# Pairing half of the third window's h before the other half is copied, in an octonion feed-forward kernel

## The chip, the cores and the metric

The kernel runs on one core of a Trainium2 chip. The metric is the device time of one execution in microseconds (us). The engines are TensorE (PE, matmuls), VectorE (DVE), ScalarE (ACT), GpSimd (POOL), and SyncE (SP), which here only issues DMAs. Each engine works through its own instructions in order; between engines there are semaphores.

## The reference

The input x has 32 sequences of 64 rows with 1024 features. Each sequence picks one of 16 matrices of 64x64, which mixes its 64 rows. The result y goes through a feed-forward layer with weights that are quantised to -1, 0 and 1 times a scale and that act as octonion products (8 parts of 128 features; the hidden width is 2728, 8 parts of 341), and x is added at the end:

```python
def oct_ternary_linear(xp, W):
    Wq = ternary_dequant(W)
    M = jnp.einsum('jik,jod->koid', S_OCT, Wq)
    return jnp.einsum('...id,koid->...ko', xp, M)
...
y = einsum('bct,bcd->bdt', x, weights[condition])
gate = oct_ternary_linear(y, w_gate); up = oct_ternary_linear(y, w_up)
h = jax.nn.silu(gate) * up
x = x + oct_ternary_linear(h, w_down)
```

## The kernel before, in words

The 2048 rows are worked through in 8 tiles T of 256 rows. The 341 hidden rows of a part are cut into three windows w of 128, 128 and 85. A tile has 12 chunks c (4 per window); a chunk makes the h of two of the eight octonion parts (v = 0 and v = 1) for one window. Chunks 8 to 11 are the third window. Every operand of the big matmuls is split into two fp16 values, a high part (ACT) and a low part (DVE).

**Gate and up.** For each chunk PE multiplies y with the gate and up tables (L1240, in the third window L1248), DVE adds the shared parts, ACT applies the silu, DVE makes h (L1083, L1047). In the third window the product comes out with rows and columns exchanged, so PE turns h (turn, L1304) two chunks later. ACT then copies h twice (split_h): the high part into h_op (L762), and the fp32 value into h_f (L767), which counts the semaphore h_copied up by one per chunk. DVE makes the low part of h (h_lo, L988).

**Rounds of z.** The down product needs, beside h itself, sums of h, called z. There are six rounds k per tile: k = 2w + v takes the four chunks of window w, half v. pair_up (L469) forms four pairings of 256 columns, of chunks 0 and 1 of the window (a = 0) and of chunks 2 and 3 (a = 1), each as a sum and a difference (r0 = 0, 1); two of them go out as one instruction of 512 columns where the signs agree, which they do for v = 1 and not for v = 0 (of the first window and the third, among others). Then two instructions of 512 columns form the sum and the difference of the pairings (L684, L685). All these are tensor_tensor instructions that a helper records at L617 on POOL and at L895 on DVE. POOL does rounds 0 to 4 of each tile (round_of_z, L672). It waits for the copy of all four chunks of the window (h_copied, L674), for the end of its last round (z_ready, L676), then pairs; it waits for the pairings (L678) and for z's buffer z_f to be free (z_lo_ready, L680), then makes z. Round 5 is done by DVE (last_round_of_z, L997), with the buffers pu_sb and z_dve. ACT makes z's high part (z_hi, L782), DVE its low part (z_lo, L995). In tiles 0 to 6 both take round 4 first and round 5 then; in the last tile round 5 first (last_rounds, L461).

**Order at the end of a tile.** ACT: the copies of chunks 10 and 11, the high part of the next tile's y (y_hi, L746), z_hi of the last two rounds, then a copy out of the down product's banks (L832). DVE: z_lo of round 3, h_lo of chunks 10 and 11, round 5, z_lo of rounds 4 and 5, the low part of the next y (y_lo, L979), the scaled addition of the down product to the residual (add_down, L1093, counts c_added), then mix_down (L1108, counts wd_ready). PE (down, L1440): for both halves s of the rows the products of windows 0 and 1 with h (down_c) and z (down_u), then those of the third window, z's last, all recorded at L1401. Then comes the next tile's first chunk (own, L1329), which writes the banks that add_down reads and so waits for c_added (L1333). In the last tile (last_down, L1414) PE does z's part of the third window and then, for the second half, all products with h. POOL ends a tile with back (L528), which adds the mixed parts to the output in SBUF; SP stores it and loads the next residual. In tile 0 POOL also mixes weights and sums y ahead of round 4 (L698 to L701).

The wait for z at the third window's product is L1465 (L1432 in the last tile); for rounds 0 to 3, z_lo_ready is awaited at L1456 (L1424).

Of the kernel before, what the change touches and what calls it, by code (L numbers as in the profile page):

```python
# [75 lines left out]
def parity(n):  # L76

    return -1 if bin(n).count("1") % 2 else 1
# [81 lines left out]
def build(nc, x, cond, cond_w, w_gate, w_up, w_down, out, count):  # L160
# [7 lines left out]
    NC = len(CHUNKS)  # L168
    NU = NC // 2
    NR = 2 * NQ  # L170
# [56 lines left out]
    with ExitStack() as ctx:  # L227
        def sb(name, shape, dt):
            return ctx.enter_context(nc.sbuf_tensor(name, shape, dt))

        def sem(name):
            return ctx.enter_context(nc.semaphore(name))
# [11 lines left out]
        h_pairs = sb("h_pairs", [P, 2, 2, TOK], F32)  # L244
# [193 lines left out]
        h_copied = sem("h_copied")  # L438
        h_lo_ready = sem("h_lo_ready")
        pairs_ready = sem("pairs_ready")  # L440
        z_ready = sem("z_ready")
# [24 lines left out]
        def z_of(k):  # L466
            return (z_dve if k == NR - 1 else z_f)[0:ROWS[k // 2]]

        def pair_up(add, k, pairs):  # L469
            w, v = divmod(k, 2)  # L470
            n_rows = ROWS[w]
            for r0 in range(2):
                signs = [KAPPA[2 * a + 1 + 4 * v] * parity(r0) for a in range(2)]
                a_runs = [(slice(0, 2), signs[0])] if signs[0] == signs[1] else [
                    (slice(a, a + 1), signs[a]) for a in range(2)]
                for a, sign in a_runs:
                    c = 4 * w + 2 * a.start
                    n = a.stop - a.start
                    op = add(pairs[0:n_rows, a, r0, :], h_f[0:n_rows, c:c + 2 * n - 1:2, v, :],
                             h_f[0:n_rows, c + 1:c + 2 * n:2, v, :], sign)  # L480
            return op
# [122 lines left out]
        def _(pool):  # L604
# [11 lines left out]
            def signed_add(dst, a, b, sign):  # L616
                return pool.tensor_tensor(dst, a, b, ALU.add if sign > 0 else ALU.subtract)  # L617
# [53 lines left out]

            def round_of_z(T, k):  # L672
                n = (NR - 1) * T + k
                pool.wait_ge(h_copied, NC * T + 4 * (k // 2) + 4)  # L674
                if n > 0:
                    pool.wait_ge(z_ready, n)  # L676
                pair_up(signed_add, k, h_pairs).then_inc(pairs_ready, 1)
                pool.wait_ge(pairs_ready, n + 1)  # L678
                if k > 0:
                    pool.wait_ge(z_lo_ready, NR * T + k)  # L680
                elif T > 0:
                    pool.wait_ge(z_lo_ready, NR * T)
                z, pairs = z_of(k), h_pairs[0:ROWS[k // 2]]
                signed_add(z[:, 0:2], pairs[:, 0], pairs[:, 1], 1)  # L684
                signed_add(z[:, 2:4], pairs[:, 0], pairs[:, 1], -1).then_inc(z_ready, 1)  # L685
# [4 lines left out]
            for T in range(NT):  # L690
                if T > 0:
                    for s in range(SUB):
                        back(pool, T - 1, s)
                if T == 0:
                    mix_down_weights(0)
                    mix_down_weights(1)
                    pool.wait_ge(slots_built[1], NQ * NBUILD)
                    for k in range(4):  # L698
                        round_of_z(T, k)
                    sum_y(1)  # L700
                    round_of_z(T, 4)  # L701
                    continue
                if T + 1 < NT:
                    sum_squares(T + 1)
                round_of_z(T, 0)
                round_of_z(T, 1)
                if T + 1 < NT:
                    sum_y(T + 1)
                for k in range(2, NR - 1):
                    round_of_z(T, k)  # L710
# [182 lines left out]
        def _(dve):  # L893
# [103 lines left out]
            def last_round_of_z(T):  # L997
                dve.wait_ge(h_copied, NC * (T + 1))
                dve.wait_ge(h_ready, NC * (T + 1))
                pair_up(signed_add, NR - 1, pu_sb).then_inc(pairs_ready_dve, 1)  # L1000
                dve.wait_ge(pairs_ready_dve, T + 1)
                z, pairs = z_of(NR - 1), pu_sb[0:LAST]
                signed_add(z[:, 0:2], pairs[:, 0], pairs[:, 1], 1)
                signed_add(z[:, 2:4], pairs[:, 0], pairs[:, 1], -1).then_inc(z_ready_dve, 1)
# [525 lines left out]
```

## Time and profile before

| what | us |
|---|---|
| median of 3 runs | 682.19 |
| lowest and highest run | 680.11, 682.54 |
| the profiled execution | 679.68 |
| its span, first to last instruction | 677.9 |
| PE busy | 639.2 (94%) |
| DVE busy | 513.9 (76%) |
| POOL busy | 386.0 (57%) |
| ACT busy | 323.6 (48%) |
| mean granted clock of PE | 0.993 |

A busy time is the time in which the engine has an instruction under way. Matmuls overlap, so a busy PE is one with no gap that shows. A row of a timeline has the start, the time taken, the engine, the line, the operation, what it writes and reads, how often, and in brackets the idle time before it and what ended that.

### The profile page before, as it was taken

How to read it: one execution, taken by the hardware profiler on the slowest of the kernel's cores; microseconds unless marked ns; L12 is line 12 of the kernel's file. 1: busy time of each engine (PE TensorE's matmuls, PEld its weight loads, DVE VectorE, ACT ScalarE, POOL GpSimd, SP SyncE). 2: the span in 40 equal slices, each digit the busy share in tenths (PEclk: the TensorE clock that was granted, in tenths of full speed). 3: DMA queues.
4: the chain of work that ended last, by engine and by line, in shares of the span. 5: the costliest groups of instructions: out<-in, count | busy, mean ns of one | idle time of the engine just before them, and what ended most of it. 6: DMA issues, size and time to landing. Idle time of an engine off the chain costs nothing. (4 is left out here: it accounts for less than half of the span.)

```text
span 677.9 us, 17119 instructions
## 1 busy us (share of the span) xinstructions
PE 639.2 (94%) x7010; PEld 592.4 (87%) x7010; DVE 513.9 (76%) x873; ACT 323.6 (48%) x542; POOL 386.0 (57%) x453
## 2 busy tenths in 40 slices
PE   3599988899999999999999999999999999999995
PEld 3378888799999999998998999999999989988995
DVE  1899975868877687767878687767878688787786
ACT  4847545255544546254553455355452544535441
POOL 1256397547647576358656476375863486464563
PEclk9799999999999999999999999999999999999999
DMA  8200030040002200032001300032000300011001
GB/s 344 67 2 1 1 131 1 33 159 3 2 1 95 99 2 1 2 125 67 2 2 42 150 2 2 1 105 88 1 2 3 125 1 2 2 62 64 2 1 63
DMA packets 10576, 31.50 MB, mean 46 GB/s; under 512 B 3330, under 2 KB 3330, under 8 KB 10370
## 3 DMA queue, kind: packets, MB, share of 16 engines
q1 hardware_dynamic: 9906, 28.81, 12.1%
q10 hardware_dynamic: 592, 1.61, 0.7%
q8 instruction: 55, 0.90, 0.5%
q14 instruction: 23, 0.19, 0.1%
HBM read 22.02 MB, written 8.39 MB: 45 GB/s over the span
## 5 line engine op out<-in xcount | busy, mean ns | idle before, releaser
L1240 PE MATMUL ps<-y_op,gate_table 128*128 128x256 f16 x1408 | 181.5, 274 | 10.7 <-DVE y_op L979 4.2
L1240 PE MATMUL ps<-y_op,up_table 128*128 128x256 f16 x1408 | 179.8, 273 | 0.3 <-ACT up_table L724 0.3
L1240 PEld LDWEIGHTS ps<-y_op,gate_table 128*128 128x128 f16 x1408 | 137.6, 98 | 29.6 <-issue 6.1
L617 POOL TENSOR_TENSOR h_pairs<-h_f 128x256 f32<-128x256 f32 (+2 forms) x128 | 119.8, 965 | 67.5 <-ACT h_f L767 54.6
L1240 PEld LDWEIGHTS ps<-y_op,up_table 128*128 128x128 f16 x1408 | 137.7, 98 | 16.6 <-DVE up_table L895 0.7
L524 POOL TENSOR_TENSOR o_sb<-o_sb,wd_sb 128x256 f32<-128x256 f32 (+1 forms) x150 | 87.5, 619 | 89.7 <-DVE wd_sb L1108 88.6
L617 POOL TENSOR_TENSOR z_f<-h_pairs 128x512 f32<-128x512 f32 (+1 forms) x80 | 102.2, 1298 | 36.5 <-DVE z_op L995 34.5
L1248 PE MATMUL ps<-third_table,y_op 128*128 128x170 f16 x1408 | 108.2, 237 | 0.5 <-ACT third_table L724 0.5
L1248 PEld LDWEIGHTS ps<-third_table,y_op 128*128 128x128 f16 x1408 | 105.1, 97 | 1.0 <-issue 0.7
L822 ACT ACTIVATE ps<-ps,small 128x512 f32<-128x512 f32 x64 | 42.4, 662 | 107.6 <-DVE ps L1009 81.6
L1401 PE MATMUL ps<-down_u,z_op 128*128 128x256 f16 (+1 forms) x768 | 90.1, 273 | 3.3 <-DVE z_op L995 3.3
L1401 PE MATMUL ps<-down_c,h_op 128*128 128x128 f16 (+1 forms) x1536 | 92.1, 219 | 1.1 <-DVE pu_sb L1047 1.1
L1401 PEld LDWEIGHTS ps<-down_c,h_op 128*128 128x128 f16 (+1 forms) x1536 | 88.8, 98 | 1.9 <-issue 1.3
L895 DVE TENSOR_TENSOR pu_sb<-ps,q_sb 128x170 f32<-128x170 f32 (+1 forms) x128 | 64.8, 506 | 33.5 <-PE ps L1240 14.2
L1401 PEld LDWEIGHTS ps<-down_u,z_op 128*128 128x128 f16 (+1 forms) x768 | 73.8, 98 | 11.7 <-DVE z_op L995 3.8
L988 DVE TENSOR_TENSOR h_op<-ps,h_op 128x512 f16<-128x512 f32 (+1 forms) x96 | 65.7, 685 | 21.8 <-ACT h_f L767 21.7
L995 DVE TENSOR_TENSOR z_op<-z_f,z_op 128x1024 f16<-128x1024 f32 (+1 forms) x40 | 49.6, 1240 | 38.9 <-ACT z_op L782 38.8
L762 ACT ACTIVATE h_op<-ps 128x512 f16<-128x512 f32 (+1 forms) x96 | 57.3, 597 | 31.1 <-DVE ps L1083 30.6
L782 ACT ACTIVATE z_op<-z_f 128x1024 f16<-128x1024 f32 (+1 forms) x40 | 42.1, 1054 | 36.4 <-POOL z_f L617 36.4
L767 ACT ACTIVATE h_f<-ps 128x512 f32<-128x512 f32 (+1 forms) x96 | 57.6, 600 | 0.0
L1083 DVE SCALAR_TENSOR_TENSOR ps<-pu_sb,small,ps 128x512 f32<-128x512 f32 x64 | 48.3, 755 | 8.1 <-ACT ps L822 2.0
L1009 DVE TENSOR_TENSOR pu_sb<-ps,pu_sb 128x512 f32<-128x512 f32 x48 | 32.9, 685 | 19.5 <-PE ps L1240 19.4
(98 smaller groups left out, 640.6 us busy)
## 6 DMA issues: line engine op xcount, KB each, us to landing
x_in<-in_x_dram SPq DMA_DIRECT2D x8, 1024.0 KB, 5.2
o_sb<-in_x_dram SPq DMA_DIRECT2D x16, 512.0 KB, 3.6
out_dram<-o_sb SPq DMA_DIRECT2D x15, 512.0 KB, 2.7
h_op<-in_L_ffn_w_gate_dram ACTq DMA_DIRECT2D x3, 512.0 KB, 6.6
h_op<-in_L_ffn_w_up_dram SPq DMA_DIRECT2D x3, 512.0 KB, 7.3
z_op<-in_L_ffn_w_down_dram SPq DMA_DIRECT2D x1, 1536.0 KB, 11.3
out_dram<-o_sb SPq DMA_DIRECT2D x2, 256.0 KB, 3.1
cond_bd<-in_L_cond_weights_dram SPq DMA_DIRECT2D x30, 16.0 KB, 2.9
```

The source lines that it names most:

```text
L524: last = eng.tensor_tensor(dst, dst, wd_sb[:, s, k1, r0, h, :], ALU.add if sign > 0 else ALU.subtract)
L617: return pool.tensor_tensor(dst, a, b, ALU.add if sign > 0 else ALU.subtract)
L762: act.activation(h_op[rows, c, :, 0, :], h_bank(c), ACT.Copy).then_inc(h_hi_ready, 1)
L767: act.activation(h_f[rows, c], h_bank(c), ACT.Copy).then_inc(h_copied, 1)
L822: act.activation(bank_r(s, 0), bank_r(s, 0), ACT.Silu, scale=gate_scale(T)).then_inc(silu_ready, 1)
L895: return dve.tensor_tensor(dst, a, b, ALU.add if sign > 0 else ALU.subtract)
L988: dve.tensor_tensor(h_op[rows, c, :, 1, :], h_bank(c), h_op[rows, c, :, 0, :], ALU.subtract).then_inc(h_lo_ready, 1)
L995: dve.tensor_tensor(z_op[rows, k, 1], z_of(k), z_op[rows, k, 0], ALU.subtract).then_inc(z_lo_ready, 1)
L1083: dve.scalar_tensor_tensor(out=bank_r(s, 0), in0=u_sb[:], scalar=up_scale(T), in1=bank_r(s, 0), op0=ALU.mult, op1=ALU.mult).then_inc(h_rea ...
L1240: mm = pe.matmul(dst, table[m][:, slot, q, :], y_op[:, op, e, :], start=(i == 0 and e == 0), stop=(i == len(terms) - 1 and e == 1))
L1248: mm = pe.matmul(dst, y_op[:, op, e, P * s:P * s + P], third_table[:, slot].rearrange("p m r -> p (m r)"), start=(i == 0 and e == 0), stop ...
L1401: mm = pe.matmul(banks[bank][:, place], operand[:, P * s:P * s + P], weights, start=(bank not in begun), stop=(last and i == ends[bank]), ...
```

## The change

In round k = NR - 2 = 4 (the third window, v = 0) POOL waits for the copy of the first two of the window's four chunks and for its last round's end, pairs those two chunks (a = 0, two instructions), then waits for the last two chunks and pairs them (a = 1, two instructions). pair_up takes the parts to do as an argument. All other rounds stay, and so does DVE's round 5.

```diff
-        def pair_up(add, k, pairs):
+        def pair_up(add, k, pairs, parts=(0, 1)):
             w, v = divmod(k, 2)
             n_rows = ROWS[w]
             for r0 in range(2):
                 signs = [KAPPA[2 * a + 1 + 4 * v] * parity(r0) for a in range(2)]
-                a_runs = [(slice(0, 2), signs[0])] if signs[0] == signs[1] else [
-                    (slice(a, a + 1), signs[a]) for a in range(2)]
+                a_runs = [(slice(0, 2), signs[0])] if signs[0] == signs[1] and len(parts) == 2 else [
+                    (slice(a, a + 1), signs[a]) for a in parts]
...
             def round_of_z(T, k):
                 n = (NR - 1) * T + k
-                pool.wait_ge(h_copied, NC * T + 4 * (k // 2) + 4)
-                if n > 0:
+                if k == NR - 2:
+
+                    pool.wait_ge(h_copied, NC * T + NC - 2)
                     pool.wait_ge(z_ready, n)
-                pair_up(signed_add, k, h_pairs).then_inc(pairs_ready, 1)
+                    pair_up(signed_add, k, h_pairs, (0,))
+                    pool.wait_ge(h_copied, NC * T + NC)
+                    pair_up(signed_add, k, h_pairs, (1,)).then_inc(pairs_ready, 1)
+                else:
+                    pool.wait_ge(h_copied, NC * T + 4 * (k // 2) + 4)
+                    if n > 0:
+                        pool.wait_ge(z_ready, n)
+                    pair_up(signed_add, k, h_pairs).then_inc(pairs_ready, 1)
                 pool.wait_ge(pairs_ready, n + 1)
```

## Rows read from the trace of the kernel before

**Rows 1.** The page, its first part: busy us (share of the span) and instructions.
```profile
PE 639.2 (94%) x7010; PEld 592.4 (87%) x7010; DVE 513.9 (76%) x873; ACT 323.6 (48%) x542; POOL 386.0 (57%) x453
```

**Rows 2.** Waits of PE, from 150 to 643 us, then from 643: total, times, longest.
```profile
PE ps L1240 <- issue: 1.2, 6, 0.2
...
PE ps L1401 <- DVE z_op L995: 2.0, 1, 2.0
```

**Rows 3.** Timeline of PE at the end of tile 6: start, us, engine, line, operation.
```profile
579.22 1.91 PE L1401 MATMUL ps<-down_u,z_op 128*128 128x256 f16 x16
...
591.61 3.66 PE L1401 MATMUL ps<-down_u,z_op 85*128 85x256 f16 x32
595.47 1.91 PE L1240 MATMUL ps<-y_op,gate_table 128*128 128x256 f16 x16 [0.20 <-issue]
```

**Rows 4.** Timeline of DVE at the end of tile 6.
```profile
587.57 1.22 DVE L995 TENSOR_TENSOR z_op<-z_f,z_op 85x1024 f16<-85x1024 f32 x1 [3.47 <-ACT z_op L782]
...
593.97 1.40 DVE L1093 SCALAR_TENSOR_TENSOR o_sb<-ps,small,o_sb 128x512 f32<-128x512 f32 x2
```

**Rows 5.** Timeline of ACT in tile 6: the copy of chunk 9, z_hi of round 4.
```profile
572.23 0.58 ACT L767 ACTIVATE h_f<-ps 85x512 f32<-85x512 f32 x1
...
586.48 1.06 ACT L782 ACTIVATE z_op<-z_f 85x1024 f16<-85x1024 f32 x1 [3.64 <-POOL z_f L617]
```

**Rows 6.** Timeline of POOL in tile 6, z of round 3, then round 4.
```profile
573.78 2.50 POOL L617 TENSOR_TENSOR z_f<-h_pairs 128x512 f32<-128x512 f32 x2 [3.07 <-DVE z_op L995]
...
579.38 0.72 POOL L617 TENSOR_TENSOR h_pairs<-h_f 85x256 f32<-85x256 f32 x1 [3.10 <-ACT h_f L767]
...
580.07 1.22 POOL L617 TENSOR_TENSOR h_pairs<-h_f 85x256 f32<-85x256 f32 x1
...
582.38 1.17 POOL L617 TENSOR_TENSOR h_pairs<-h_f 85x256 f32<-85x256 f32 x1
...
583.63 1.60 POOL L617 TENSOR_TENSOR z_f<-h_pairs 85x512 f32<-85x512 f32 x1
...
585.19 1.26 POOL L617 TENSOR_TENSOR z_f<-h_pairs 85x512 f32<-85x512 f32 x1
```

**Rows 7.** Timeline of DVE in tile 6, from z_lo of round 3 to round 5.
```profile
577.40 1.23 DVE L995 TENSOR_TENSOR z_op<-z_f,z_op 128x1024 f16<-128x1024 f32 x1 [0.87 <-ACT z_op L782]
...
579.40 0.69 DVE L988 TENSOR_TENSOR h_op<-ps,h_op 85x512 f16<-85x512 f32 x1 [0.18 <-ACT h_f L767]
580.01 0.68 DVE L895 TENSOR_TENSOR pu_sb<-h_f 85x512 f32<-85x512 f32 x1
...
580.61 1.22 DVE L895 TENSOR_TENSOR pu_sb<-h_f 85x512 f32<-85x512 f32 x1
...
582.89 1.21 DVE L895 TENSOR_TENSOR h_f<-pu_sb 85x512 f32<-85x512 f32 x1
```

**Rows 8.** Timelines at the end of tile 0: ACT's last copy, POOL's round 4, PE.
```profile
105.40 0.60 ACT L767 ACTIVATE h_f<-ps 85x512 f32<-85x512 f32 x1
...
108.45 4.13 POOL L617 TENSOR_TENSOR h_pairs<-h_f 85x256 f32<-85x256 f32 x4
...
124.16 1.91 PE L1240 MATMUL ps<-y_op,gate_table 128*128 128x256 f16 x16 [1.82 <-issue]
```

**Rows 9.** The last tile: chain of waits (first row, start, us, what), then timelines.
```profile
653.61 0.02 POOLq L680
...
657.88 2.84 POOL L617 TENSOR_TENSOR z_f<-h_pairs 85x512 f32<-85x512 f32 x2
...
658.39 1.06 ACT L782 ACTIVATE z_op<-h_f 85x1024 f16<-85x1024 f32 x1 [4.82 <-DVE h_f L895]
...
659.48 2.32 DVE L995 TENSOR_TENSOR z_op<-h_f,z_op 85x1024 f16<-85x1024 f32 x1 [1.12 <-ACT z_op L782]
661.84 1.22 DVE L995 TENSOR_TENSOR z_op<-z_f,z_op 85x1024 f16<-85x1024 f32 x1
...
663.12 3.67 PE L1401 MATMUL ps<-down_u,z_op 85*128 85x256 f16 x32 [1.95 <-DVE z_op L995]
```

## The prediction

> **What bounds the kernel now.** I read the page first: TensorE (PE) is busy for 639.2 us, 94% of a span of 677.9 us [rows 1]. So only time in which PE stands still can be saved. The view of waits, for PE alone and by stretch, says where that is behind the first tile: between 150 and 643 us it idles six times by 0.2 us, at the first matmul of a tile (L1240), and in the last stretch once by 2.0 us, for VectorE's (DVE's) z_op, the low part of z (L995) [rows 2]. The first tile has its own gaps, among them 1.82 us before tile 1. The six short gaps are one pattern, once per tile; I follow the one ahead of the last tile.
>
> The gap of 0.20 us counts from the modelled end of the last matmul. Sixteen such matmuls of 0.273 us take 1.91 us, so one follows another by (1.91 - 0.27) / 15 = 0.109 us; the 32 from 591.61 would make room for the next at 595.10, and it starts at 595.47 [rows 3]. **Each gap is really worth 0.37 us**, and the wait of 1.95 us in the last tile 1.95 + 0.27 - 0.11 = 2.11 us.
>
> What ends the short gap the trace calls "issue". I read it from DVE's timeline: the low parts of z from 587.57, behind them y's low parts, and behind those, up against them, the residual's first addition, at 593.97 + 1.40 = 595.37, 0.10 us before PE goes on [rows 4]. In the code L1333 has PE wait for just this (c_added), since the addition reads the banks that the next tile's first chunk writes. DVE had come late because it stood idle up to 587.57 for ScalarE's (ACT's) copy at 586.48, and ACT had waited 3.64 us for POOL's z [rows 4, 5]. So POOL's round 4 sets the tile's border.
>
> **What the change moves.** Round 4 has four pairings of 85x256 and two z instructions of 85x512, before and after; the two signs differ for v = 0, so no run is split by the new parts. Only their order changes, and one wait more stands between the second and third pairing. Chunk 9 is copied at 572.23 + 0.58 = 572.81 [rows 5]. POOL's z of round 3 ends at 573.78 + 2.50 = 576.28, then it idles until the copy of chunk 11 releases it at 579.38 [rows 6]. Two pairings fit into that hole: from 576.36, 0.72 us for one, they end at about 577.8.
>
> They do not simply come off the path, because **POOL and DVE take turns** in instructions that read two operands from SBUF. Look at 580 us: DVE's pairing runs 580.01 to 580.69, POOL's, started at 580.07, ends at 581.29, that is 0.60 us after DVE's; DVE's next, started at 580.61, ends at 581.83, 0.54 us after POOL's. POOL's pairing to 583.55, DVE's to 584.10, POOL's z to 585.23 [rows 6, 7]: each time the later one ends its own working time (POOL 0.59 for a pairing, 1.13 for a z; DVE 0.55) after the other has finished. In the last tile DVE's z_lo, 1.22 us when alone, takes 2.32, and ends 1.08 us after POOL's z does at 660.72 [rows 9].
>
> With these turns I lay out a middle tile:
> - POOL: pairings 1 and 2 in the hole; 3 from 579.38 to 580.10, 4 to 581.29 as the second one now; then z at once, from 581.37, held to 581.83, done 582.96; second z, held by DVE to 583.51, done **584.64 instead of 586.45**: 1.8 us earlier, where two pairings as they stand are 1.17 each, 2.3 us.
> - DVE's own last round (k = 5): its third and fourth instruction are now held by z instructions of 1.13 instead of pairings of 0.59. They end at 583.51 and **585.19 instead of 584.10**: 1.1 us later. ACT's copy of round 4 (from 584.68) hides that: round 5's comes about 1 us after it.
> - DVE then starts z_lo of round 4 at 585.8 instead of 587.57, and the addition ends at 593.6, well before PE's 595.10. The gap closes; the cap is PE itself, so of 1.8 us only 0.37 counts. Six borders: **-2.2 us** (0.20 x 6 = 1.2 is the least, if my reading of the modelled ends is off).
> - Cost on the way: z_lo of round 3 (577.40) is held to 577.8 and ends at 578.85 instead of 578.63. PE needs it at 579.22 [rows 3, 7]: a margin of 0.37 us covers it, 0 us. If the cover goes, each later tenth costs a tenth in each of six tiles. The low part of h behind it reads PSUM; the one at 579.40 was not held by the pairing at 579.38 [rows 6, 7].
> - The added wait costs POOL an instruction of its own at most, and the chain of waits has one at 0.02 us [rows 9]. Queued behind it are POOL's last two pairings and z, with ACT and DVE behind those, which needed chunk 11 before too. 0 us, at most 0.1 on the last tile's path. No DMA is issued or passed by POOL; the stores on SP's queue come 1 to 2 us earlier and nobody waits for them.
> - The first tile: chunk 11 is copied by 106.0, and POOL, late with other sums, begins round 4 at 108.45. Both waits are passed there, only the order changes; the 1.82 us before tile 1 stays [rows 8]. 0 us, within 0.1 either way for one more wait.
>
> **The last tile** is where the chain of waits runs through POOL, and where one expects the most. But there DVE finishes round 5 first (last_rounds is reversed). The same turns, 74.25 us later (from 583.63 to 657.88, where POOL's z starts): DVE's round ends at 659.44 instead of 658.35, ACT's copy of it 660.55 instead of 659.45 [rows 6, 9]. POOL is done by 658.9, so DVE's z_lo at 660.58 is no longer held: 1.22 us instead of 2.32, it ends at 661.80, exactly as before. Round 4's copy by ACT is over by 661.6; its z_lo can start right behind, at 661.72 instead of 661.84. Gain: **-0.1 us** of the 2.11. The bounds are +1.1 (the round lost, nothing given back) and -2.11 (the wait gone).
>
> The Trainium skill has a rule that speaks against a gain here: "SBUF — State Buffer", section "Who interferes with whom", has the pair of ports that VectorE and GpSimd share as an exclusive lock for a whole instruction, taken by whoever issues first, when VectorE has two SBUF inputs. By that rule the last tile gives nothing, as the durations in this trace do; were it a split of bandwidth it would give 1.2 us.
>
> **Sum.** -2.2 - 0.1 = -2.3 us. The profiled execution took 679.68 us (span 677.9), so 677.4 by it. That execution lay 2.5 us below the median of the three runs, 682.19 (they reach from 680.11); the same difference from the median gives **679.9 us**. About 0.5%, 3.4 us, is what a measurement of this kernel can tell from no change: the forecast is within it.
>
> **Rivals.**
> 1. *The last tile gains too.* DVE gets its turns sooner than I have it, its round ends at 658.4 and its z_lo at 660.7, then 661.9: 1.2 us off, up to 2.1. For it: the chain that ended last goes through all four pairings and both z. Against: strict turns in every pair of rows. Sum -3.4 to -4.3: 678.8 to 677.9 us. Chance 0.16.
> 2. *Nothing moves.* The trace names no releaser of the six gaps; were it PE's own start of the new tile, DVE's 1.8 us would be hidden. Against: the end of the addition leads PE by 0.10 us, and the code has the wait. Or the early pairings never start early, since z_ready comes with the end of round 3: only if that wait lasts to 579. 682.1 us. Chance 0.14.
> 3. *Slower: DVE loses its turn and POOL wins nothing.* If POOL's z still ends near 660 in the last tile (because of the added wait, or of its pairings being held by z_lo of round 3), DVE's round 5 ends 1.1 us later, its z_lo is still held, and PE waits 1.1 us longer, while the borders stay open: 683.3 us. It decides from the point where POOL's last z ends later than 660.6, when z_lo starts. Against: the hole is 3.1 us for 1.4 us of work. Chance 0.08. Slower by over 0.5% needs, on top of it, z_lo of round 3 past its margin of 0.37 us in all tiles.
>
> My forecast keeps 0.62. Faster by over 0.5%: most of rival 1 and a little scatter, 0.20; slower by over 0.5%: 0.04; within: 0.76. Range: from 677.6 (rival 1, and a little scatter) to 682.6 (rival 2 and half of rival 3's loss).
>
> **What would show it.** Right: POOL's pairings in two groups of two, the first from about 576.4 in the tile that I followed; z done 1.8 us earlier; PE's six idle times of 0.2 us gone from its waits, and each tile from the second on 0.37 us shorter; DVE's round 5 ending 1.1 us later; and in the last tile PE still idle for about 1.9 us ahead of the down product of z. Wrong: the last idle time down to 1 us or less (rival 1), the six gaps in place (rival 2), a new wait of PE for DVE's z_lo in the second window's product (the margin was not enough).

## The result and the profile after

The changed kernel takes 679.7 us (median of 22 runs, 676.87 to 680.7), the kernel before, run beside it, 681.11 (22 runs). The ratio is 0.9976 with a 95% interval of 0.9968 to 0.9984: 1.6 us faster, between 1.1 and 2.2, and within the 0.5% that the prediction called no change. The forecast was 679.9 us, 2.3 us off a median of 682.19.

A run's mean granted clock of PE is the clock that the chip granted it, as a share of the full 2.4 GHz, averaged over the run. It is on record for 64 runs of the kernel before (those beside the experiments below, and its repetition) and for the 22 of the changed kernel, and the runs fall into groups by it. The groups are a better ruler than the medians (one slow run of the kernel before, 690.48 us at a clock of 0.941, is left out):

| mean granted clock | before: runs, us | median | changed: runs, us | median |
|---|---|---|---|---|
| 0.981 to 0.982 | 19, 681.6 to 682.9 | 682.0 | 11, 679.3 to 680.7 | 680.1 |
| 0.985 to 0.987 | 9, 681.2 to 683.4 | 681.7 | 3, 679.5 to 679.8 | 679.8 |
| 0.988 to 0.991 | 28, 679.6 to 680.9 | 680.4 | 8, 676.9 to 678.5 | 678.2 |
| 0.993 | 8, 679.4 to 679.8 | 679.6 | none | |

Within a group the change is worth about 1.9 to 2.2 us, though the clocks of the two kernels in a group are close and mostly not the same. What a kernel's median is depends also on how its runs spread over the groups.

**The borders between the tiles.** In the view of waits of PE, from 150 to 643 us, the changed kernel has no row at all: the six idle times of 0.2 us [rows 2] are gone. Its timelines at the end of tile 6 (start, us, engine, line, operation; lines from L682 on are 8 higher than before), POOL first:

```profile
573.68 2.50 POOL L617 TENSOR_TENSOR z_f<-h_pairs 128x512 f32<-128x512 f32 x2 [3.07 <-DVE z_op L1003]
576.33 1.41 POOL L617 TENSOR_TENSOR h_pairs<-h_f 85x256 f32<-85x256 f32 x2
579.28 1.92 POOL L617 TENSOR_TENSOR h_pairs<-h_f 85x256 f32<-85x256 f32 x2 [1.54 <-ACT h_f L775]
581.28 3.28 POOL L617 TENSOR_TENSOR z_f<-h_pairs 85x512 f32<-85x512 f32 x2
...
577.30 1.52 DVE L1003 TENSOR_TENSOR z_op<-z_f,z_op 128x1024 f16<-128x1024 f32 x1 [0.88 <-ACT z_op L790]
...
581.79 3.33 DVE L903 TENSOR_TENSOR h_f<-pu_sb 85x512 f32<-85x512 f32 x2
585.69 1.22 DVE L1003 TENSOR_TENSOR z_op<-z_f,z_op 85x1024 f16<-85x1024 f32 x1 [0.58 <-ACT z_op L790]
...
592.09 1.40 DVE L1101 SCALAR_TENSOR_TENSOR o_sb<-ps,small,o_sb 128x512 f32<-128x512 f32 x2
...
591.51 3.66 PE L1409 MATMUL ps<-down_u,z_op 85*128 85x256 f16 x32
595.00 1.91 PE L1248 MATMUL ps<-y_op,gate_table 128*128 128x256 f16 x16
```

This execution is 0.10 us ahead of the one before here (PE's z product at 591.51 for 591.61, [rows 3]). POOL's pairings stand in two groups, with the hole between them. z is done at 581.28 + 3.28 = 584.56 for 586.45, DVE's round 5 at 585.12 for 584.10, and the addition, up to 595.37 before [rows 4], ends at 593.49. PE goes on at 595.00, 3.49 us after 591.51: 32 times 0.109, no gap.

What the six gaps gave can be read from the two traces directly. From the second group of products of tile 1, where both are at full clock, to the first of tile 7 the kernel before takes 595.47 - 125.91 = 469.56 us, with this row as its start, and the changed one 595.00 - 127.61 = 467.39: 2.17 us less, six times 0.36.

```profile
125.91 1.91 PE L1240 MATMUL ps<-y_op,up_table 128*128 128x256 f16 x16
```

**The last tile.** The same views:

```profile
653.18 1.91 POOL L617 TENSOR_TENSOR h_pairs<-h_f 85x256 f32<-85x256 f32 x2 [1.55 <-ACT h_f L775]
655.17 3.27 POOL L617 TENSOR_TENSOR z_f<-h_pairs 85x512 f32<-85x512 f32 x2
...
655.68 3.31 DVE L903 TENSOR_TENSOR h_f<-pu_sb 85x512 f32<-85x512 f32 x2
660.11 1.22 DVE L1003 TENSOR_TENSOR z_op<-h_f,z_op 85x1024 f16<-85x1024 f32 x1 [1.12 <-ACT z_op L790]
661.25 1.21 DVE L1003 TENSOR_TENSOR z_op<-z_f,z_op 85x1024 f16<-85x1024 f32 x1
...
658.75 1.95 PE L1409 MATMUL ps<-down_c,h_op 85*128 85x128 f16 x32
662.53 6.16 PE L1409 MATMUL ps<-down_u,z_op 85*128 85x256 f16 x32 [1.82 <-DVE z_op L1003]
668.48 6.39 PE L1409 MATMUL ps<-down_c,h_op 128*128 128x128 f16 x96
```

z_lo of round 5 runs in 1.22 us instead of 2.32 [rows 9], but DVE's z of round 5 takes 3.31 instead of 2.2, and PE still idles for 1.82 us, where it idled for 1.95. POOL's z is done at 655.17 + 3.27 = 658.44, where it was 660.72; this execution is 0.46 us ahead at the copy of chunk 11 (POOL starts at 653.18, before at 653.64), so 1.8 us of that are the change's. The last tile hardly gains by it.

The last two rows hold what the prediction did not have: PE's 32 products take 6.16 us, before 3.67 [rows 9]. The view by stretches, from 662 to 670 us, gives the granted clock (the 0.59; busy times of PE, PEld, DVE, ACT, POOL before it), between the full 2.4 GHz and 1.2; before it was 1.00 there:

```profile
662.00:670.00 8.00, 7.47 (x47) 5.92 (x48) 3.70 (x6) 1.37 (x2) 2.36 (x4) 0.59 0.01 2
```

The clock was low at the start of tile 1 as well (0.76 in the stretch from 123 to 130 us, before 1.00). There the first 16 products take 3.50 us:

```profile
124.28 3.50 PE L1248 MATMUL ps<-y_op,gate_table 128*128 128x256 f16 x16 [1.82 <-issue]
127.61 1.91 PE L1248 MATMUL ps<-y_op,up_table 128*128 128x256 f16 x16
```

Both have a price. The first is 3.33 us from 124.28 to 127.61 for the 1.75 that such a group takes at full clock (595.00 to 596.75), 1.6 us. The second shows from the start of z's product to the end of the span: 678.3 - 662.53 = 15.8 us, before 677.9 - 663.12 = 14.8, so 1.0 us. The profiled execution took 680.12 us; less 2.6 that is 677.5, where the prediction had 677.4. A third low stretch, 0.83 from 100 to 110 us (before 1.00), costs little: tile 1 starts at 124.28 for 124.16.

### The profile page after: what moved, and what is told of

Read it like the earlier page. It is cut to its first block and busy times, and to the rows that moved or that the text cites. A ratio compares the mean times of both kernels' runs of the same rounds, so it can differ in the third digit from the quotient of the medians.

```text
span 678.3 us, 17119 instructions
## 1 busy us (share of the span) xinstructions
PE 644.8 (95%) x7010; PEld 596.8 (88%) x7010; DVE 522.1 (77%) x873; ACT 323.3 (48%) x542; POOL 383.2 (56%) x453
## 5 line engine op out<-in xcount | busy, mean ns | idle before, releaser
L617 POOL TENSOR_TENSOR h_pairs<-h_f 128x256 f32<-128x256 f32 (+2 forms) x128 | 113.9, 916 | 59.0 <-ACT h_f L775 45.1
L617 POOL TENSOR_TENSOR z_f<-h_pairs 128x512 f32<-128x512 f32 (+1 forms) x80 | 105.3, 1336 | 36.6 <-DVE z_op L1003 34.7
L1409 PE MATMUL ps<-down_u,z_op 128*128 128x256 f16 (+1 forms) x768 | 93.3, 278 | 1.8 <-DVE z_op L1003 1.8
L1409 PE MATMUL ps<-down_c,h_op 128*128 128x128 f16 (+1 forms) x1536 | 94.0, 221 | 1.1 <-DVE pu_sb L1055 1.1
L1409 PEld LDWEIGHTS ps<-down_c,h_op 128*128 128x128 f16 (+1 forms) x1536 | 90.6, 99 | 2.0 <-issue 1.3
L1409 PEld LDWEIGHTS ps<-down_u,z_op 128*128 128x128 f16 (+1 forms) x768 | 75.3, 100 | 11.5 <-DVE z_op L1003 2.0
L1003 DVE TENSOR_TENSOR z_op<-z_f,z_op 128x1024 f16<-128x1024 f32 (+1 forms) x40 | 51.7, 1291 | 21.4 <-ACT z_op L790 21.4
```

The lines of the kernel that those rows point to most:

```text
L1003: dve.tensor_tensor(z_op[rows, k, 1], z_of(k), z_op[rows, k, 0], ALU.subtract).then_inc(z_lo_ready, 1)
L1409: mm = pe.matmul(banks[bank][:, place], operand[:, P * s:P * s + P], weights, start=(bank not in begun), stop=(last and i == ends[bank]), ...
```

## The experiments

My theory A: six borders give 0.37 us each, because DVE's addition comes earlier; the last tile gives nothing, because POOL and DVE take turns. The rivals: B, the last tile gives the time; C, the low clock belongs to the new order; D, PE waits at the border for something else, or the change has a gain beside the gaps; E, POOL is slow in the last tile for itself; F, against C, the clock falls now and then in either kernel. Ratios are to the kernel before, run beside them.

**Where the gain is: the change cut in two.**

```diff
-                if k == NR - 2:
+                if k == NR - 2 and T == NT - 1:
```

> The changed kernel with the new order of round 4 in the last tile alone. Theory A (the gain is at the six tile borders, the last tile gives nothing because POOL and DVE take turns): ratio 0.9995 to 1.000, 0 to 0.1 us; PE's six idle times of 0.20 us stay; in the last tile POOL's pairings stand in two groups, DVE's round 5 ends about 1.1 us later, PE still idles 1.8 to 2.0 us before z's last product. Theory B (the last tile gives what the change saves, 1.2 to 2.1 us): ratio 0.997 to 0.998, PE's idle time there under 1 us.

Measured: 679.96 us, 0.9984 (0.9973 to 0.9996). The waits of PE between 150 and 640 us keep the gaps, and the last tile looks as in the changed kernel.

```profile
PE ps L1248 <- issue: 1.2, 6, 0.2
```

The timelines of its last tile:

```profile
652.99 1.91 POOL L617 TENSOR_TENSOR h_pairs<-h_f 85x256 f32<-85x256 f32 x2 [1.55 <-ACT h_f L775]
...
655.49 3.31 DVE L903 TENSOR_TENSOR h_f<-pu_sb 85x512 f32<-85x512 f32 x2
...
662.34 5.50 PE L1409 MATMUL ps<-down_u,z_op 85*128 85x256 f16 x32 [1.82 <-DVE z_op L1003]
```

Theory A's trace, and 0.13 us of idle time gained. The ratio is lower than expected, and its interval reaches B's 0.997 to 0.998: none of its 12 runs had a clock of 0.982, and 9 of the 21 of the kernel before had. Runs of 0.990 are 679.95 to 680.27 against 680.12 to 680.52, and the medians at 0.986, 0.990 and 0.993 lie about 0.3 us apart. B is out by the trace, which has 1.82 us of idle time where B had under 1, and by these runs.

```diff
-                if k == NR - 2:
+                if k == NR - 2 and T < NT - 1:
```

> The changed kernel with the new order of round 4 in every tile but the last. Theory A: all of the gain, 2.2 us, ratio 0.9968; the six idle times of PE at the start of a tile are gone, the last tile is as before (POOL's four pairings in one group, PE idle for 1.95 us). Theory B: less than 1 us, ratio over 0.9985. Theory C (a lower granted clock at the end or after tile 0 comes with the new order and eats part of the gain): if it hangs on the last tile's new order, the clock near the end is full again here.

Measured: 679.75 us, 0.9974 (0.9963 to 0.9985), the whole of the change's gain; a little less than the 2.2 us that I expected, within the interval. No idle row between 150 and 640 us. In the last tile POOL works as before and the clock falls all the same:

```profile
652.48 4.16 POOL L617 TENSOR_TENSOR h_pairs<-h_f 85x256 f32<-85x256 f32 x4 [3.10 <-ACT h_f L775]
...
661.94 6.43 PE L1409 MATMUL ps<-down_u,z_op 85*128 85x256 f16 x32 [1.94 <-DVE z_op L1003]
```

So the fall does not hang on the last tile's new order.

```diff
-                if k == NR - 2:
+                if k == NR - 2 and T > 0:
```

> The changed kernel with the new order of round 4 in tiles 1 to 7, tile 0 as before. Theory A (tile 0 gets nothing from the change, since chunk 11 is copied long before POOL comes to round 4): the same as the changed kernel, ratio 0.9966 to 0.9976. Theory C (the falls of PE's granted clock at about 103 and 124 us in the changed kernel's trace come from tile 0's new order): they are gone here, and the ratio is 0.2% lower.

Measured: 678.54 us, 0.9967 (0.995 to 0.9983); the changed kernel's interval overlaps it. In this execution the clock was full from 100 to 110 us and at the start of tile 1, and low at the end (0.50 from 662 to 670). But among its 11 runs are three with a clock of 0.981 or 0.982, at 679.46 to 680.49, like the changed kernel's. One full stretch in one execution doesn't decide on C, and the times don't tell it apart; the next run says more.

**Does the low clock belong to the change?** The kernel before, once more:

> The kernel before once more, for a second trace and for the scatter. Theory F (the granted clock falls at the same few places in any of these kernels, now and then): ratio 1.000 within 0.001; the six idle times of 0.20 us are there again; and if this execution is one with a lower mean clock than 0.993, the falls stand near 103 to 127 us and after 660 us, as in the changed kernel. Theory C (those falls belong to the change): none there.

Measured: 680.86 us, 1.0001 (0.9986 to 1.0016). Its profiled execution took 681.71 us, at a mean clock of 0.982. The view of waits from 150 to 640:

```profile
PE ps L1240 <- issue: 1.1, 6, 0.2
```

PE's timeline in the last tile, and after it the view of the stretch from 662 to 670:

```profile
662.54 7.01 PE L1401 MATMUL ps<-down_u,z_op 85*128 85x256 f16 x32 [1.95 <-DVE z_op L995]
```

```profile
662.00:670.00 8.00, 7.46 (x39) 5.50 (x40) 3.21 (x5) 1.10 (x2) 1.49 (x3) 0.53 0.01 2
```

The same code, after the same wait of 1.95 us, ran these products in 3.67 us the first time and in 7.01 now. The view of 100 to 110 us has 0.83, as the changed kernel's has. So the low clock at these two places is met in either kernel, and C is out for them; what decides between low and full is open. At the start of tile 1 this execution had the full clock. Of the traces in which PE idles for 1.82 us there, three of the five with the new order in tile 0 have the low clock behind it, and none of the four without. Of the changed kernel's 22 runs 11 are in the slowest group of the table and none in the fastest, of the kernel before 19 and 8 of 64. Both point to falls that come more often with the change; neither settles it.

**Is it the addition that PE waits for at a border?** DVE's addition moved ahead, POOL untouched (in the kernel before):

```diff
-                    y_lo(T + 1)
-                if T + 1 < NT:
-                    for s in range(SUB):
-                        add_down(T, s)
+                    y_lo(T + 1, range(2))
+                    add_down(T, 0)
+                    y_lo(T + 1, range(2, NY))
+                    add_down(T, 1)
```

> The kernel before, with DVE's first addition of the down product moved ahead of the last third of y's low part; POOL as before. Theory A (PE's idle time at a tile border waits for that addition, 0.37 us at six borders, and at the border after tile 0 most of 1.98 us): the addition ends 1.8 us earlier, all seven gaps close, 2.2 + 1.7 = 3.9 us, ratio 0.9943. Theory D (PE waits there for y or for something of its own): the gaps stay, ratio 1.000.

Measured: 676.51 us, 0.9926 (0.9912 to 0.994). In the waits from 100 us on, all seven gaps at L1241 are missing; the second fence has the timelines of DVE and PE at the first border:

```profile
PE ps L1305 <- DVE odd_h_sb L1047: 2.1, 1, 2.1
PE ps L1402 <- DVE z_op L995: 1.9, 1, 1.9
```

```profile
121.22 1.40 DVE L1093 SCALAR_TENSOR_TENSOR o_sb<-ps,small,o_sb 128x512 f32<-128x512 f32 x2
122.53 1.80 DVE L979 SCALAR_TENSOR_TENSOR y_op<-y_f,small,y_op 128x1536 f16<-128x1536 f32 x1
...
122.72 1.91 PE L1241 MATMUL ps<-y_op,gate_table 128*128 128x256 f16 x16
```

PE starts tile 1 at 122.72, 0.10 us after the addition's end, where it did at 124.16 [rows 8]. It isn't y that it waited for: y's last third (DVE's row from 122.53) is under way when PE starts, up to 124.33. D's first half is out: PE waits for this addition. Two runs at a clock of 0.993 took 675.55 and 675.63 us, 4.0 less than the kernel before at that clock, for the 3.9 expected. The ratio itself says 5.0 us, more than the 0.9943 expected: at the lower clocks the difference is larger, 676.06 us against 680.12 to 680.52 at 0.990, and 676.96 to 677.16 at 0.984 against 681.63 to 682.38 at 0.982.

The same edit in the changed kernel:

> The changed kernel with DVE's first addition moved ahead of the last third of y's low part. Theory A (both edits close the same six gaps, which can be closed but once): against the kernel with that addition moved alone (ratio 0.9926) only the last tile's 0.1 us are added, ratio 0.992 to 0.993. Theory D (the change has a gain of its own beside the gaps): another 1.5 to 2 us, ratio 0.990.

Measured: 676.2 us, 0.9946 (0.9925 to 0.9966), five runs spread over four clocks; the 0.992 to 0.993 that I expected is at the interval's edge. At 0.993 it took 675.31, 0.2 to 0.3 us less than the same edit without the change, and at 0.990 676.2 for 676.06. The gaps can be closed only once: beside the moved addition the change is worth next to nothing, and D's second half, another 1.5 to 2 us, is out.

**Are the turns real?** DVE's round 5 taken out of the last tile (z of round 5 isn't computed there; one instruction of one column stands for it):

```diff
+                if T == NT - 1:
+                    dve.tensor_scalar(warm_dve, scale[0], 1.0, None, ALU.mult).then_inc(z_ready_dve, 1)
+                    return
                 pair_up(signed_add, NR - 1, pu_sb).then_inc(pairs_ready_dve, 1)
```

> The changed kernel without DVE's round 5 in the last tile (four instructions left out, one of one column in their place; z of round 5 there is not computed). Theory A (turns between POOL and DVE): POOL's last pairing takes 0.72 us instead of 1.2, its two z instructions 2.5 us together instead of 3.27, so z of round 4 is done 1.2 us earlier after chunk 11's copy (4.0 us instead of 5.3), and z_lo runs in 1.22 us. PE's idle time before z's last product falls from 1.8 to under 0.2 us. Theory E (POOL is slow there for itself, by its own waits): POOL's times stay at 1.2 and 3.27.

Measured: 677.2 us in a single run. The timelines:

```profile
653.28 1.41 POOL L618 TENSOR_TENSOR h_pairs<-h_f 85x256 f32<-85x256 f32 x2 [1.54 <-ACT h_f L776]
654.77 3.47 POOL L618 TENSOR_TENSOR z_f<-h_pairs 85x512 f32<-85x512 f32 x2
...
655.21 1.91 DVE L1004 TENSOR_TENSOR z_op<-h_f,z_op 85x1024 f16<-85x1024 f32 x1 [1.12 <-ACT z_op L791]
...
658.85 1.95 PE L1413 MATMUL ps<-down_c,h_op 85*128 85x128 f16 x32
660.64 3.67 PE L1413 MATMUL ps<-down_u,z_op 85*128 85x256 f16 x32
```

The pairings take 1.41 us instead of 1.91: alone, they are 0.7 each. POOL's z did not fall to 2.5 us as I had written: with round 5 gone, z_lo of round 5 came forward, to 655.21, took its turn between the two z instructions, and was itself held, 1.91 us instead of 1.22. A miss of my expectation (POOL's z is done 5.0 us after chunk 11's copy, not 4.0), and one more instance of turns: here z_lo holds POOL's z as round 5 did. POOL slow for itself (E) is out, by the pairings. PE's wait before z is gone.

**The last tile's order.** Round 4 first there too:

```diff
-            return ks if T + 1 < NT else ks[::-1]
+            return ks
```

> The changed kernel, with ACT and DVE taking round 4 ahead of round 5 in the last tile too. Theory A, by the turns laid out from the trace: ACT copies round 4's z about 0.5 us before DVE's round 5 ends, DVE's two low parts end about 0.5 us earlier, PE idles about 1.3 us instead of 1.8 there: 0.5 us better than the changed kernel, ratio to the kernel before 0.9960 at equal clock. Theory B (DVE's round 5 is what PE waits for, whatever the order): no difference from the changed kernel, idle 1.8 us.

Measured: 677.51 us, 0.996 (0.9945 to 0.9976). The timelines of the last tile:

```profile
653.54 3.31 DVE L903 TENSOR_TENSOR h_f<-pu_sb 85x512 f32<-85x512 f32 x2
657.42 1.22 DVE L1003 TENSOR_TENSOR z_op<-z_f,z_op 85x1024 f16<-85x1024 f32 x1 [0.57 <-ACT z_op L790]
...
659.83 3.67 PE L1409 MATMUL ps<-down_u,z_op 85*128 85x256 f16 x32 [1.26 <-DVE z_op L1003]
```

PE's wait is 1.26 us instead of 1.82, as expected. In its four runs at 0.989 the median is 677.44, for 678.18 of the changed kernel at that clock: 0.7 us, a little more than the 0.5 expected. The reversed order fits the kernel before, where POOL's z came last (round 4 first was not run there), and no longer once POOL has gained and DVE lost.

**The wait filled.** 32 of the second half's products with h are put into it:

```diff
                 down_part(0, down_c_of(2), False, True).then_inc(down_c_done, 1)
+                for w in range(2):
+                    down_part(1, down_c_of(w, (0,)), w == 0, False, ("c0",))
                 pe.wait_ge(z_lo_ready, n + NR)
...
-                    for w in range(NQ):
+                    for w in range(0 if h else 2, NQ):
```

> The changed kernel with 32 of the second half's down products (1.8 us) put into PE's wait before z's last product in the last tile, and nothing else. Theory A: PE's work after z is 1.8 us shorter, DVE's tail (mix_down, the two passes into the output, the last addition) is not; at full clock the end moves by 0 to 0.3 us, at the low clock by up to 3 us since the products behind z are what the low clock stretches: ratio 0.995 to 0.9965, and the scatter of the runs shrinks. If the end is not bound by PE in the slower runs: ratio as the changed kernel, 0.9976.

Measured: 677.05 us, 0.9946 (0.9928 to 0.9964), and five of six runs lie between 677.0 and 677.32. In its timeline PE goes from one group to the next with no idle time that shows:

```profile
656.68 3.74 PE L1409 MATMUL ps<-down_c,h_op 85*128 85x128 f16 x64
660.45 3.67 PE L1409 MATMUL ps<-down_u,z_op 85*128 85x256 f16 x32
```

The 64 products from 656.68 take 3.77 us up to the next group, where the same 64 in tile 6 of the changed kernel take 3.58 (587.93 to 591.51), and DVE's last z_lo ends at 660.39: PE still waited for it, by 0.2 us. From z's product to the end it is 675.2 - 660.45 = 14.8 us, as in the kernel before at full clock, though PE has 1.8 us less to do there: at full clock PE does not set that end, and the 0 to 0.3 us expected of it don't show. What the filling may have bought is the clock: four of its six runs have a mean of 0.992, and the changed kernel has none above 0.989. With six runs that the filling keeps the clock up is likely, not shown.

**All of it**: the changed kernel with the moved addition, round 4 first, and the filled wait.

> The changed kernel with three more edits: the addition ahead of the last third of y, round 4 first in the last tile, and two thirds of the second half's first down products (32 matmuls, 1.8 us) put into PE's wait before z's last product. Theory A: borders as before_add_ahead_of_y3 (0.9926), the last tile 0.5 us better from the order; the filled wait shortens PE's work at the end by 1.3 us, of which DVE's tail behind it lets through 0.3 us at full clock and over 1 us where the clock is low. Ratio 0.9905 to 0.992. If PE's products only come later for it: 0.993.

Measured: 675.39 us (674.86 to 675.7), 0.992 (0.9902 to 0.9938): 5 us below the kernel before and, by the ratios, nearly 4 below the changed one, a version that beats both. Most of it is the moved addition, which alone gave 0.9926 (0.9912 to 0.994) in the kernel before; that the other edits add to it isn't shown, since the intervals overlap. In its last tile the filling is now too long: z_lo ends at 657.44 + 1.21 = 658.65 and PE comes to z at 659.07, 0.4 us late, which fewer products would mend (not tried). DVE's and PE's timelines there:

```profile
657.44 1.21 DVE L1003 TENSOR_TENSOR z_op<-h_f,z_op 85x1024 f16<-85x1024 f32 x1
...
659.07 3.66 PE L1410 MATMUL ps<-down_u,z_op 85*128 85x256 f16 x32
```

## Why the prediction was right, point by point

- **What bounds the kernel**: right. "Issue" at the border is the wait for c_added; moving that one addition closes all seven gaps, with nothing else changed.
- **The turns of POOL and DVE**: right, and to within 0.07 us when the 0.10 us of lead are added: POOL's z 584.66 for 584.64, DVE's round 5 585.22 for 585.19, the addition 593.6 for 593.6, z_lo of round 3 at 578.92 for 578.85. The Trainium skill's rule ("SBUF — State Buffer", "Who interferes with whom"), an exclusive lock held for the whole instruction, agrees with each of these rows. The prediction does not show how it came to 1.2 us in the last tile for a split of the bandwidth; the idle time there fell by 0.13.
- **Six borders, 2.2 us**: right. The trace has none of the gaps, the stretch with them is 2.17 us shorter, and the change without the last tile has the whole gain. The margin of z_lo of round 3 held: PE shows no wait from 150 to 643 us.
- **The last tile, 0.1 us**: right, 0.13 (idle 1.95 to 1.82); the runs of the change in the last tile alone say about 0.3.
- **Tile 0, nothing**: right as to the order: the 1.82 us before tile 1 stay, and without the new order in tile 0 the ratio is no worse (0.9967 for 0.9976, within the intervals). Not foreseen was the low clock behind that wait, 1.6 us in the profiled execution.
- **The sum**: 2.3 us forecast, 1.6 measured (1.1 to 2.2), 1.9 to 2.2 within a group of clocks, and 2.17 + 0.12 = 2.3 in the two traces apart from the clock (from tile 7's start to z's last product 67.65 us before, 67.53 after). The term that is missing is PE's clock: I had taken all durations from an execution with a mean of 0.993, the fastest group of the kernel before, and none of the 22 runs of the changed kernel is in it. That the spread over the groups covers the rest of the gain is likely, not shown. My estimate of the median (679.9 for 679.7) is luck: the median before was itself 681.11 and not 682.19 in the larger series, and 2.3 us off that is 678.8.
- **Rivals**: 1 and 2 fell by the two halves of the change; of 3 one half happened. DVE's round was pushed back by 1.1 us, and that was given back in z_lo.

## What to carry to other kernels

When an engine's work is moved earlier, lay out on paper which instructions of the other engine will now meet it: here the saved pairings of 0.6 us gave their place to z instructions of 1.1, and DVE paid for it just where its result is read next. An idle time that the profile calls "issue" is read from the code's wait and from what ended 0.1 us before it; the cheapest cure was to move the one instruction that is awaited ahead of one that isn't awaited yet. After a gain on one side, look again at an order that was chosen by who came last.

## What the runs showed of the hardware that I had not expected

The granted clock of PE is not the same in two executions of one program: after the same wait of 1.95 us, 32 products took 3.67 us in one and 7.01 in another (granted clock 0.53 from 662 to 670 us, between 2.4 and 1.2 GHz).

The twelve traces of this study, one for each run, show the clock below full in four places, each behind an idle time of PE. From 27 to 35 us it is 0.67 to 0.87 in all twelve, behind 4.2 us; from 100 to 110 us 0.83 in seven, behind 2.1 us; from 123 to 130 us 0.76 in three of the nine that idle for 1.8 us there; from 662 to 670 us 0.50 to 0.68 in six of the eight that idle for 1.8 to 1.95 us ahead of z's last product, and full in the four that idle there for 1.26 us or not at all. From 150 to 643 us, where PE never idles for more than 0.2 us, it is 1.00 in all twelve. These are single executions of different kernels: that the idle time brings the fall is likely, and why it does so in one execution and not in the next is open.

So a short wait of PE late in a kernel can cost its own length and, in some executions, up to 2.6 us more: 17.4 us from z's product to the end in the kernel's second trace (679.9 - 662.54), 14.8 in its first.
